# A two-layer graph attention kernel: the first x chunks cut to 2, 2, 4 and then 8 tiles, and three of them rectified at once

## The chip, the cores and the metric

One core of one Trainium2 chip. The metric is device time of the whole kernel in microseconds (us), the median of several runs. Engines are named as the profile names them: PE (TensorE), PEld (its weight loads), ACT (ScalarE), DVE (VectorE), POOL (GpSimd), SP (the queue that issues most DMAs).

## The reference

Two graph attention layers over 8192 nodes with 256 features and a dense int32 adjacency matrix of 8192 x 8192.

```
h  = relu(layernorm(x));  Wh = h @ W
e  = (Wh @ a_left)[:, None] + (Wh @ a_right)[None, :]
x1 = x + leaky_relu(softmax(where(adj, e, -inf), axis=1) @ Wh, 0.2)      # layer 0
h  = relu(layernorm(x1))
out = x1 + softmax(where(adj, leaky_relu(h@a_l + (h@a_r).T), -inf)) @ h  # layer 1
```

In layer 0 the left score falls out of the softmax, so a row of attention weights is the adjacency mask times one weight per key, exp(score of the key minus the largest score).

## The kernel before, in words

The 8192 rows of x are 64 tiles of 128. The part that the change touches is the opening of layer 0, which has four stages and ends when the largest score is known.

**Loading.** SP loads x into HV in chunks of tiles, two DMAs for each chunk (L330, every other tile each). `EDGES` holds the chunk borders: 0, 2, 8, 16, ... 64, nine chunks. Chunk c >= 4 is issued when chunk c-4 has landed. Between chunk 0 and the rest SP issues the weights W (L334), the attention row (L335) and the identity (L337), and all three count on one semaphore, `w_in`. After the chunks come six constants and one row of h. Then SP loads the adjacency matrix in quarters of a tile (L358), each when ACT has converted the quarter that was in its buffer.

**Normalising.** DVE computes `statistics(c)`: a bn_stats for each tile of the chunk (L610) and then a bn_aggr for each (L615). ACT takes the roots of the variances (`roots(c)`, L463). DVE's `scales(c)` makes 1/std (L620) and -mean/std (L623), and ACT's `relus(c)` (L477) writes relu of the normalised tile, tile by tile. ACT's order is: roots(0), relus(0), roots(1), and then for c = 2 to 8 roots(c) followed by relus(c-1), and relus(8) last. In front of relus(7) it also loads the table of Exp (L495). DVE's order is: statistics(0), scales(0), `score_columns` (L593, L595: the identity as bf16, and W times the attention row as an extra column of W), statistics(1), scales(1), statistics(2), and then statistics(c), scales(c-1) for c = 3 to 8; scales(8) stands in the loop that follows.

**Projecting.** PE runs, for t = 0 to 63, `transpose_h(t)` (L980, two transposes) and then `project(t-1)` (L989, four matmul records of 128x257, with the score as an extra column). `relus` has a copy of the transposed tile t-2 (`copy_hT`, L470) behind the relu of tile t. So ACT's order is relu t, copy t-2, relu t+1, copy t-1. DVE copies each projection out of PSUM (`take_wh(t)`, L603). Inside the statistics the copy of tile t-TAKE stands behind the bn_stats of tile t; TAKE is 24. There are three PSUM buffers for projections, so project(t) waits for take_wh(t-3). Behind the relus of tiles 28, 32, ... 56 ACT converts a quarter of adjacency (L458), eight in all. DVE folds the converted masks of two tiles into words (L642 to L656), behind take_wh(43) and take_wh(59), and PE turns them (L1001) after transpose 50 and at the end.

**Weighting.** When the last projection is copied, DVE reduces the scores, POOL finds the largest (its L424), ACT takes the exponentials (L512), and ACT and DVE make the weighted values of the 64 tiles (L519, L703). PE's first aggregation (L1016) follows this tile by tile. After that PE runs the aggregation of 64 row tiles, with conversions, folds and lists beside it. Layer 1 follows.

PE starts with two waits, on `w_in` and on `ucol_ready` (the score columns in W).

Of the kernel before, what the change touches and what calls it, by code (L numbers as in the profile page):

```python
# [35 lines left out]
def two_layer_graph_attention(nc, x, adj, w0, a0, a1, key_pos, ident, tri, caps, row_ids, self_pos, out):  # L36
# [30 lines left out]
    P = 128  # L67
    N, D = x.shape
    T = N // P
# [10 lines left out]
    Q = 4  # L80
    QC = N // Q
    QB = QC // P
    XC = 8
    EDGES = [0, 2] + list(range(XC, N // P + 1, XC))
    NCH = len(EDGES) - 1
    TAKE = 24
    XB = 4
    LAG = 5
    XL = 1
# [47 lines left out]
    with outer:  # L137
# [13 lines left out]
        with ctx:  # L151
# [99 lines left out]
            ucol_ready = sem("ucol_ready")  # L251
# [64 lines left out]
            SPARSE, DENSE = SP0, -NS  # L316

            CONVERTS = list(range(T - 2 * Q * 4 - 4, T - 4, 4))
            FOLDS = {CONVERTS[Q - 1] + 3: 0, CONVERTS[2 * Q - 1] + 3: 1}

            def offset(t):
                return SPARSE if t < NS else DENSE
# [2 lines left out]
            def _(sp):  # L325
                def load_chunk(c):
                    if c >= XB:
                        sp.wait_ge(x_in[c % XB], c // XB * 32)
                    for h in range(2):
                        sp.dma_start(H[:, EDGES[c] + h:EDGES[c + 1]:2, 0:D],  # L330
                                     x_v[:, EDGES[c] // 2:EDGES[c + 1] // 2, h, :]).then_inc(x_in[c % XB], 16)

# [117 lines left out]
            def _(act):  # L450
# [10 lines left out]
                def roots(c):  # L461
                    act.wait_ge(mv_ready, EDGES[c + 1])
                    nc.scalar.activation(std[:, EDGES[c]:EDGES[c + 1]], mv[:, EDGES[c]:EDGES[c + 1], 1],  # L463
                                         ACT.Sqrt, bias=eps[:, :]).then_inc(std_ready, 1)
# [8 lines left out]
                def relus(c):  # L473

                    act.wait_ge(nmr_ready, c + 1)
                    for t in range(EDGES[c], EDGES[c + 1]):
                        nc.scalar.activation(H[:, t, 0:D], H[:, t, 0:D], ACT.Relu,  # L477
                                             scale=rstd[:, t:t + 1],
                                             bias=nmr[:, t:t + 1]).then_inc(h_ready, 1)
                        if t >= 2:  # L480
                            copy_hT(t - 2)
                        if t in CONVERTS:
                            k = CONVERTS.index(t)
                            convert(k // Q, k // Q, [k % Q], True)

                act.wait_ge(ones_set, 1)
                nc.scalar.activation(std1[:, :], eps[:, :], ACT.Sqrt, bias=eps[:, :]).then_inc(warm, 1)
                roots(0)
                relus(0)
                roots(1)  # L490
                for c in range(2, NCH):
                    roots(c)
                    if c == NCH - 1:
                        act.wait_ge(warm, 1)
                        nc.scalar.activation(std1[:, :], eps[:, :], ACT.Exp).then_inc(warm, 1)  # L495
                    relus(c - 1)
                relus(NCH - 1)
                copy_hT(T - 2)
                copy_hT(T - 1)
# [79 lines left out]
                for j in range(NX):  # L579
                    t = last * NX + j  # L580
# [8 lines left out]
            def _(dve):  # L589
# [15 lines left out]
                def statistics(c):  # L605
                    dve.wait_ge(x_in[c % XB], 32 * (c // XB + 1))
                    if c:
                        dve.wait_ge(mv_ready, EDGES[c])
                    for t in range(EDGES[c], EDGES[c + 1]):
                        nc.vector.bn_stats(st[:, t % XC, :], H[:, t, 0:D]).then_inc(st_ready, 1)  # L610
                        if t >= TAKE:
                            take_wh(t - TAKE)
                    for t in range(EDGES[c], EDGES[c + 1]):
                        dve.wait_ge(st_ready, t + 1)
                        nc.vector.bn_aggr(mv[:, t, :], st[:, t % XC, :]).then_inc(mv_ready, 1)  # L615
# [10 lines left out]
                statistics(0)  # L626
                scales(0)
                score_columns()
                statistics(1)
                scales(1)  # L630
                dve.wait_ge(ones_set, 2)
                for c in range(2, NCH):
                    statistics(c)
                    if c > 2:
                        scales(c - 1)
                def fold(t, b, part):

# [38 lines left out]

                for t in range(T - TAKE, T - TAKE + XC - 2):
                    take_wh(t)
# [20 lines left out]
                with dve.Fori(0, T // VU) as k:  # L699
                    for j in range(VU):  # L700
                        t = k * VU + j
# [268 lines left out]
            @block.tensor  # L970
            def _(pe):
                pe.wait_ge(w_in, 16 * 3)
                pe.wait_ge(ucol_ready, 2)

                def transpose_h(t):
                    pe.wait_ge(h_ready, t + 1)
                    if t >= 2:
                        pe.wait_ge(hT_ready, t - 1)
                    for c in range(2):
                        last = nc.tensor.transpose(tps[t % 2][:, c * P:(c + 1) * P],  # L980
                                                   H[:, t, c * P:(c + 1) * P], idf[:, :])
                    last.then_inc(tr_ready, 1)

                def project(t):
                    pe.wait_ge(hT_ready, t + 1)
                    if t >= 3:
                        pe.wait_ge(wh_ready, t - 2)
                    for c in range(2):
                        last = nc.tensor.matmul(wps[t % 3][:, 0:DV], hT[:, t % 2, c, :], w_sb[:, c, :],  # L989
                                                start=(c == 0), stop=(c == 1))  # L990
                    last.then_inc(proj_ready, 1)

                def turn(t, b, reuse=True):

                    pe.wait_ge(fold_ready, t * 3 + 3)
                    if reuse:
                        pe.wait_ge(pk_ready, t - 1)
                    pe.sem_inc(masks_due, 1)
                    words = fold1[:, b, 1, :].bitcast(bf16)
                    for q in range(BQ):  # L1000
                        last = nc.tensor.transpose(turned[b].bitcast(bf16)[:, q * P:(q + 1) * P],  # L1001
                                                   words[:, q * P:(q + 1) * P], idb[:, :])
                    last.then_inc(words_ps, 1)

                def aggregate(t, b, v0_wait=False, reuse=True, turn_at=T // 16):

                    pe.wait_ge(adjT_ready, t + 1)
                    if reuse:
                        pe.wait_ge(ysb_ready, t - 1)
                    pe.sem_inc(masks_due, 1)  # L1010
                    for jb in range(T):
                        if v0_wait:
                            pe.wait_ge(v0_ready, jb + 1)
                        for s in range(2):
                            q, i, h = place(jb)
                            last = nc.tensor.matmul(acc[b][:, 0:DV], adjT_h[:, b, i, q, :, h],  # L1016
                                                    V0[:, jb, s, 0:DV], start=(jb == 0 and s == 0),
                                                    stop=(jb == T - 1 and s == 1))
                        if jb == turn_at:
                            turn(t + 1, 1 - b)  # L1020
                    last.then_inc(acc_ready, 1)

                for t in range(T):
                    transpose_h(t)
                    if t >= 1:
                        project(t - 1)
                    if t == T - 14:
                        pe.wait_ge(idb_ready, 1)
                        turn(0, 0, False)
                project(T - 1)  # L1030
                turn(1, 1, False)
                pe.wait_ge(wh_ready, T)
                pe.wait_ge(ones_set, 2)
                aggregate(0, 0, v0_wait=True, reuse=False, turn_at=None)
                aggregate(1, 1, reuse=False, turn_at=3 * T // 4)
                with pe.Fori(1, SORT // 2) as k:
                    for b in range(2):
                        aggregate(k * 2 + b, b)
                for b in range(2):
                    aggregate(SORT + b, b)  # L1040
                pe.wait_ge(const_in, 16 * 6)
                pe.wait_ge(totals_ready, 1)
                nc.tensor.matmul(kps[0][:, 0:KC], trib[:, 0:P], sums2[:, 1, :], start=True, stop=False)
                nc.tensor.matmul(kps[0][:, 0:KC], trib[:, P:2 * P], sums2[:, 0, :], start=False, stop=True)\
                    .then_inc(rank_ps, 1)
                with pe.Fori(SORT // 2 + 1, T // 2 - 1) as k:
                    for b in range(2):
                        aggregate(k * 2 + b, b)
                aggregate(T - 2, 0)
                aggregate(T - 1, 1, turn_at=None)  # L1050
                pe.wait_ge(h12_kept, 3 * T - 2)
                nc.tensor.transpose(kps[1][0:T, 0:P], h1all[:, :], idf[:, :]).then_inc(h1T_ps, 1)
# [747 lines left out]
```

## Time and profile before

| what | value |
|---|---|
| median of 3 runs | 1689.78 us (1688.65 to 1690.71) |
| the profiled execution's own time | 1692.08 us |
| its span | 1689.8 us |
| busy: PE, DVE, ACT, POOL | 1551.9, 1256.5, 989.3, 564.1 us |
| mean granted TensorE clock | 0.973 |

The span begins with the first instruction and ends with the last, and the device time of the same execution is 2.3 us longer. The opening, up to the copy of the last projection, is the first 100 us of it. Layer 0's aggregation ends near 1063 us, and layer 1 fills the rest. A timeline line gives start, duration, engine, source line, operation and count; a bracket behind it gives how long the engine sat idle before it, and what released it.

### The profile page before, as it was taken

How to read it: one execution, taken by the hardware profiler on the slowest of the kernel's cores; microseconds unless marked ns; L12 is line 12 of the kernel's file. 1: busy time of each engine (PE TensorE's matmuls, PEld its weight loads, DVE VectorE, ACT ScalarE, POOL GpSimd, SP SyncE). 2: the span in 40 equal slices, each digit the busy share in tenths (PEclk: the TensorE clock that was granted, in tenths of full speed). 3: DMA queues.
4: the chain of work that ended last, by engine and by line, in shares of the span. 5: the costliest groups of instructions: out<-in, count | busy, mean ns of one | idle time of the engine just before them, and what ended most of it. 6: DMA issues, size and time to landing. Idle time of an engine off the chain costs nothing. (4 is left out here: it accounts for less than half of the span.)

```text
span 1689.8 us, 37172 instructions
## 1 busy us (share of the span) xinstructions
PE 1551.9 (92%) x13443; PEld 1323.6 (78%) x13443; DVE 1256.5 (74%) x4759; ACT 989.3 (59%) x1514; POOL 564.1 (33%) x588
## 2 busy tenths in 40 slices
PE   6877999999999999999999999486898999989896
PEld 5645888888888888888888888374687877877685
DVE  6577998998898899887874443696866667666765
ACT  5978656665765566566666661675645445444542
POOL 0000000000000000000014453587777777777776
PEclk9998999999999999999999999798999999999998
DMA  9418989888988898898889994555444444444443
GB/s 312 170 49 331 349 303 372 320 293 317 369 312 295 332 357 307 302 373 320 341 328 380 397 363 106 176 133 156 117 133 110 133 122 131 116 138 117 125 119 106
DMA packets 141700, 406.91 MB, mean 241 GB/s; under 512 B 25857, under 2 KB 91586, under 8 KB 108834
## 3 DMA queue, kind: packets, MB, share of 16 engines
q1 hardware_dynamic: 116114, 335.11, 54.1%
q0 software_dynamic: 25488, 70.77, 14.7%
q8 instruction: 28, 0.46, 0.1%
q14 instruction: 70, 0.57, 0.1%
HBM read 365.39 MB, written 40.41 MB: 240 GB/s over the span
## 5 line engine op out<-in xcount | busy, mean ns | idle before, releaser
L1016 PE MATMUL banks<-HV,adjT 128*128 128x257 f16 x8192 | 939.6, 274 | 17.1 <-DVE adjT L673 9.4
L1016 PEld LDWEIGHTS banks<-HV,adjT 128*128 128x128 fp8e4 x8192 | 792.9, 98 | 149.0 <-DVE HV L703 23.1
L1750 PE MATMUL banks<-Vp,adjp 128*128 128x257 f16 x2304 | 450.3, 277 | 80.3 <-DVE adjp L1562 64.0
L458 ACT ACTIVATE adj_f<-adj_i 128x2048 fp8e4<-128x2048 int32 x256 | 480.1, 1898 | 5.5 <-DMA adj_i<-in_adj 5.5
L1334 POOL DMA_INDIRECT gat<-h_of_layer,rec x393 | 423.0, 1076 | 121.1 <-issue 115.6
L1750 PE MATMUL banks<-Vn,adjn 128*128 128x257 f16 x2304 | 449.7, 277 | 0.0
L1750 PEld LDWEIGHTS banks<-Vp,adjp 128*128 128x128 fp8e4 x2304 | 224.5, 98 | 124.0 <-issue 61.3
L440 POOL DMA_DIRECT2D xr<-x_after_layer x46 | 25.8, 561 | 834.1 <-DVE rank L941 772.4
L1750 PEld LDWEIGHTS banks<-Vn,adjn 128*128 128x128 fp8e4 x2304 | 227.0, 99 | 36.3
L1369 ACT ACTIVATE adjn<-h1bc,nh 128x384 fp8e5<-128x384 f32 x384 | 202.4, 603 | 0.0
L1390 ACT ACTIVATE e<-gat,hb 128x4 f32<-128x4 f32 (+3 forms) x168 | 41.2, 293 | 241.9 <-DMA gat<-h_of_layer,rec 241.9
L1623 DVE SCALAR_TENSOR_TENSOR sacc<-gat,w,sacc 128x257 f32<-128x257 f32 x347 | 157.6, 480 | 0.0
L1601 DVE TENSOR_TENSOR w<-e 128x5 f32<-128x5 f32 (+2 forms) x84 | 13.7, 163 | 166.2 <-ACT e L1390 165.9
L506 ACT ACTIVATE pk<-banks 128x512 uint16<-128x512 uint16 x64 | 37.7, 589 | 137.9 <-PE banks L1001 137.8
L670 DVE TENSOR_SCALAR adjT<-pk 128x512 uint16<-128x512 uint16 x448 | 95.1, 283 | 0.0
L710 DVE RECIPROCAL rden<-banks 128x1 f32<-128x1 f32 x64 | 10.7, 168 | 109.7 <-PE banks L1016 108.5
L989 PE MATMUL banks<-w_sb,hT 128*128 128x257 f32 x256 | 69.6, 395 | 16.0 <-ACT hT L470 15.7
L642 DVE SCALAR_TENSOR_TENSOR fold<-adj_f 128x1024 int32<-128x1024 int32 x64 | 77.2, 1207 | 7.6 <-ACT adj_f L458 7.5
L539 ACT ACTIVATE hh<-x,nmr,rstd 128x256 f32<-128x256 f32 x64 | 38.5, 601 | 61.2 <-DVE nmr L742 61.2
L533 ACT ACTIVATE std<-mv,eps 128x1 f32<-128x1 f32 x64 | 18.9, 295 | 92.7 <-DVE mv L734 92.4
L547 ACT ACTIVATE ysb<-banks,rden 128x256 f32<-128x256 f32 x64 | 29.8, 466 | 72.4 <-DVE rden L710 72.4
L989 PEld LDWEIGHTS banks<-w_sb,hT 128*128 128x128 f32 x256 | 45.2, 197 | 22.8 <-ACT hT L470 18.9
(172 smaller groups left out, 1481.9 us busy)
## 6 DMA issues: line engine op xcount, KB each, us to landing
adj_i<-in_adj SPq DMA_DIRECT2D x256, 1024.0 KB, 7.3
h_of_layer<-hh SPq DMA_DIRECT2D x64, 129.0 KB, 6.9
hs<-h_of_layer SPq DMA_DIRECT2D x64, 129.0 KB, 3.3
xt<-in_x SPq DMA_DIRECT2D x64, 128.0 KB, 7.0
packed_adj<-pk SPq DMA_DIRECT2D x64, 128.0 KB, 6.7
x_after_layer<-x SPq DMA_DIRECT2D x64, 128.0 KB, 7.1
HV<-in_x SPq DMA_DIRECT2D x14, 512.0 KB, 8.8
gat<-h_of_layer,rec POOLq DMA_INDIRECT x393
```

Source lines behind the costliest of these rows:

```text
L458: nc.scalar.activation(adj_f[:, b, q * QC:(q + 1) * QC], adj_i[:, q, :], ACT.Copy, scale=2.0, saturate=False).then_inc(conv_done, 1)
L506: nc.scalar.activation(pk[:, pb, :], turned[b].bitcast(u16), ACT.Copy).then_inc(pk_ready, 1)
L539: nc.scalar.activation(hh[:, b, 0:D], x1[:, b, :], ACT.Relu, scale=rstd1[:, bass.ds(t, 1)], bias=nmr1[:, bass.ds(t, 1)]).then_inc(hh_ready, 1)
L642: nc.vector.scalar_tensor_tensor(four, whole[:, 0:4 * GW], 1, whole[:, 4 * GW:8 * GW], ALU.logical_shift_right, ALU.bitwise_or)\
L670: last = nc.vector.tensor_scalar(adjT[:, b, i, :], pk[:, pb, :], PAIR << i, 6 - i, ALU.bitwise_and, ALU.logical_shift_left)
L989: last = nc.tensor.matmul(wps[t % 3][:, 0:DV], hT[:, t % 2, c, :], w_sb[:, c, :], start=(c == 0), stop=(c == 1))
L1016: last = nc.tensor.matmul(acc[b][:, 0:DV], adjT_h[:, b, i, q, :, h], V0[:, jb, s, 0:DV], start=(jb == 0 and s == 0), stop=(jb == T - 1 and ...
L1334: pool.indirect_dma_start(gat[:, k % NBUF, s - s0, :], None, h_d, bass.IndirectOffsetOnAxis(ap=rec[:, m, s:s + 1], axis=0))\
L1369: i = nc.scalar.activation(adjn_b[:, c % AN, jb // 2, :, jb % 2], h1bc[:, g2, :], ACT.Relu, scale=-BIG, bias=nh2[:, tiles[j]:tiles[j] + 1] ...
L1390: nc.scalar.activation(e8[:, k % 2, i, 0:s1 - s0], gat[:, k % NBUF, 0:s1 - s0, DV], ACT.Exp, scale=scale, bias=hb[:, i, m:m + 1]).then_inc ...
L1623: nc.vector.scalar_tensor_tensor(acc, x, w, acc, ALU.mult, ALU.add)\
L1750: mm = nc.tensor.matmul(bank[2 * i + part][:, 0:DV], m[:, i * P:(i + 1) * P], V[:, j, s, 0:DV], start=(j == 0 and s == 0), stop=(j == T - ...
```

## The change

The chunk borders become 0, 2, 4, 8, 16, ... 64, ten chunks. `DIRECT` is 3: chunks 0, 1 and 2 (tiles 0 to 7) go through statistics, roots, scales and relus before the next chunk is looked at, on ACT and on DVE. From chunk 3 on ACT runs roots(c) ahead of relus(c-1), and DVE statistics(c) ahead of scales(c-1). `TAKE` becomes 18, so that the copy of projection t-18 stands behind the bn_stats of tile t, and the first fold stands behind take_wh(46). PE no longer waits for the score columns before the first transpose, but before the first projection.

```diff
-    EDGES = [0, 2] + list(range(XC, N // P + 1, XC))
+    EDGES = [0, 2, XC // 2] + list(range(XC, N // P + 1, XC))
     NCH = len(EDGES) - 1
-    TAKE = 24
+    DIRECT = 3
+    TAKE = 18
...
-            FOLDS = {CONVERTS[Q - 1] + 3: 0, CONVERTS[2 * Q - 1] + 3: 1}
+            FOLDS = {T - TAKE: 0, CONVERTS[2 * Q - 1] + 3: 1}
...
-                roots(0)
-                relus(0)
-                roots(1)
-                for c in range(2, NCH):
+                for c in range(DIRECT):
+                    roots(c)
+                    relus(c)
+                for c in range(DIRECT, NCH):
                     roots(c)
                     if c == NCH - 1:
                         act.wait_ge(warm, 1)
                         nc.scalar.activation(std1[:, :], eps[:, :], ACT.Exp).then_inc(warm, 1)
-                    relus(c - 1)
+                    if c > DIRECT:
+                        relus(c - 1)
                 relus(NCH - 1)
...
                 score_columns()
-                statistics(1)
-                scales(1)
+                for c in range(1, DIRECT):
+                    statistics(c)
+                    scales(c)
                 dve.wait_ge(ones_set, 2)
-                for c in range(2, NCH):
+                for c in range(DIRECT, NCH):
                     statistics(c)
-                    if c > 2:
+                    if c > DIRECT:
                         scales(c - 1)
...
                 pe.wait_ge(w_in, 16 * 3)
-                pe.wait_ge(ucol_ready, 2)
...
                         pe.wait_ge(wh_ready, t - 2)
+                    if t == 0:
+                        pe.wait_ge(ucol_ready, 2)
```

## Rows read from the trace of the kernel before

**Rows 1.** windows: stretch, length, busy us of PE, PEld, DVE, ACT, POOL (records), PE clock, DMA share, GB/s

```profile
70.00:80.00 10.00, 7.19 (x38) 5.52 (x37) 5.04 (x13) 9.77 (x18) 0.00 (x0) 1.00 0.40 129
...
100.00:110.00 10.00, 3.98 (x21) 2.21 (x19) 8.55 (x33) 6.22 (x16) 0.37 (x1) 0.71 0.00 0
```

**Rows 2.** timeline, PE, start of layer 0: start, duration, operation, [idle before it <- releaser]

```profile
16.85 2.08 PE L989 MATMUL banks<-w_sb,hT 128*128 128x257 f32 x4 [8.01 <-ACT hT L470]
...
22.88 1.03 PE L989 MATMUL banks<-w_sb,hT 128*128 128x257 f32 x4
...
27.24 1.03 PE L989 MATMUL banks<-w_sb,hT 128*128 128x257 f32 x4
```

**Rows 3.** timeline, ACT, same stretch

```profile
5.27 1.09 ACT L477 ACTIVATE HV<-HV,nmr,rstd 128x256 f32<-128x256 f32 x2 [0.51 <-DVE nmr L623]
...
15.74 0.30 ACT L463 ACTIVATE std<-mv,eps 128x8 f32<-128x8 f32 x1 [3.75 <-DVE mv L615]
15.94 0.59 ACT L477 ACTIVATE HV<-HV,nmr,rstd 128x256 f32<-128x256 f32 x1
16.43 0.36 ACT L470 ACTIVATE hT<-banks 128x256 f32<-128x256 f32 x1
...
33.35 0.59 ACT L477 ACTIVATE HV<-HV,nmr,rstd 128x256 f32<-128x256 f32 x1
```

**Rows 4.** timeline, DVE, same stretch

```profile
3.45 0.75 DVE L610 BATCH_NORM_STATS2 st<-HV 128x6 f32<-128x256 f32 x2 [3.45 <-DMA HV<-in_x]
...
5.07 0.16 DVE L623 SCALAR_TENSOR_TENSOR nmr<-mv,rstd 128x2 f32<-128x2 f32 x1
...
7.57 0.08 DVE L595 DVE_READ_ACCUMULATOR2_ANT w_sb<- 128x1 f32 x1
9.19 2.06 DVE L610 BATCH_NORM_STATS2 st<-HV 128x6 f32<-128x256 f32 x6 [1.54 <-issue]
...
15.08 0.62 DVE L615 BATCH_NORM_AGGREGATE mv<-st 128x2 f32<-128x6 f32 x8
...
28.31 0.43 DVE L603 COPY HV<-banks 128x257 f32<-128x257 f32 x1 [0.33 <-PE banks L989]
28.65 0.63 DVE L615 BATCH_NORM_AGGREGATE mv<-st 128x2 f32<-128x6 f32 x8
...
29.48 0.17 DVE L623 SCALAR_TENSOR_TENSOR nmr<-mv,rstd 128x8 f32<-128x8 f32 x1
```

**Rows 5.** timeline, PE, later part of the projections

```profile
53.41 1.03 PE L989 MATMUL banks<-w_sb,hT 128*128 128x257 f32 x4
...
55.52 1.14 PE L989 MATMUL banks<-w_sb,hT 128*128 128x257 f32 x4 [0.85 <-ACT hT L470]
...
74.22 1.03 PE L989 MATMUL banks<-w_sb,hT 128*128 128x257 f32 x4
...
76.23 1.14 PE L989 MATMUL banks<-w_sb,hT 128*128 128x257 f32 x4 [0.75 <-ACT hT L470]
...
78.79 1.14 PE L989 MATMUL banks<-w_sb,hT 128*128 128x257 f32 x4 [1.21 <-ACT hT L470]
```

**Rows 6.** timeline, ACT, before and after the table load in front of tile 48

```profile
73.61 0.29 ACT L463 ACTIVATE std<-mv,eps 128x8 f32<-128x8 f32 x1
...
75.33 0.58 ACT L477 ACTIVATE HV<-HV,nmr,rstd 128x256 f32<-128x256 f32 x1
```

**Rows 7.** timeline, DVE: a fold, and the last copy of a projection

```profile
73.46 1.21 DVE L642 SCALAR_TENSOR_TENSOR fold<-adj_f 128x1024 int32<-128x1024 int32 x1
...
76.10 0.75 DVE L603 COPY HV<-banks 128x257 f32<-128x257 f32 x2
...
99.97 0.43 DVE L603 COPY HV<-banks 128x257 f32<-128x257 f32 x1 [0.63 <-PE banks L989]
```

**Rows 8.** timeline, SP, issues of x chunks and of adjacency quarters

```profile
3.11 19.94 SPq L330 DMA_DIRECT2D HV<-in_x  x16
...
83.48 50.67 SPq L358 DMA_DIRECT2D adj_i<-in_adj  x3
```

## The prediction

> **What bounds the kernel now.** I read the windows of the opening first, for where PE is idle: it is short of work at the start, in the conversions (7.19 us busy of the ten from 70 us) and in the step to the weighted values (3.98 of the ten from 100 us) [rows 1]. The timelines say what PE waits for. Its first projection starts at 16.85, after 8.01 us of idleness that ended with ACT's copy of transposed tile 0 [rows 2]. That copy, at 16.43 [rows 3], stands behind the relu of tile 2, and that relu behind roots(2), which needs the statistics of tiles 8 to 15: their bn_aggr runs from 15.08 for 0.62 us [rows 4]. So the start is set by order on ACT and DVE, not by loading: tiles 0 and 1 were rectified from 5.27 on [rows 3].
>
> From the fourth projection (22.88) PE is the bound: four tiles from 22.88 to 27.24, 1.09 us each. The first three took 6.03 us (16.85 to 22.88) where 3.27 would do, and a projection's matmuls ran 2.08 us against 1.03: twice the time, so I read 1.2 GHz there and 2.4 GHz behind it [rows 2]. In the conversions PE waits for ACT, 0.85 us in front of 55.52 [rows 5]. DVE waits for PE at a take (0.33 us in front of 28.31), and this is slack today: take 7, the last in statistics(4), starts at 28.31 and the scales that follow are made at 29.48, while ACT reaches tile 16, which needs them, at 33.35 [rows 3, 4]. The slack is 33.35 - 29.48 - 0.20 = 3.7 us, 0.20 being the step from 5.07 to 5.27.
>
> Everything after the opening hangs on its end, the last take at 99.97 [rows 7]: largest score, weights, the values tile by tile, and with them the next loads. SP stands in an adjacency issue from 83.48 for 50.67 us, three issues in all [rows 8], because its buffer is free only when ACT converts again after the values. So I carry a shift of the end through one for one.
>
> **The change, part by part.**
>
> *Chunks 1 and 2 direct.* After the change DVE goes from the score columns (last record 7.57 + 0.08 = 7.65) to the statistics of tiles 2 and 3. From bn_stats to relu, chunk 0 took 3.45 to 5.27 = 1.82 us for two tiles [rows 3, 4]. So relu 2 starts at 7.7 + 1.8 = 9.5. The copy of tile 0 follows 0.49 later and the projection 0.42 after that (15.94 to 16.43 to 16.85): 10.4, against 16.85. **Gain 6.4 us.** This needs chunk 1 in by 7.65. No row shows a 256 KB chunk there. Bounds: all 768 KB of the old chunk were in by 9.19 [rows 4], which would cost 1.5 us; for the other end, earlier landing gains nothing, as DVE is busy until 7.65. I take 7.65, as a third of those bytes comes first. Two more issues on SP stand among sixteen that take 19.94 us, 1.25 each at most, [rows 8] with other chunks in flight; the adjacency quarters behind them are needed only by ACT's first conversion, behind the relu of tile 28. Cost 0.
>
> The Trainium skill, page "DMA: Bandwidth & Descriptors", Rules for kernel authors, advises to coalesce transfers, since each has a fixed part of about 2.0 us (its Anatomy section). Were that paid in series by both new chunks, the gain would be an estimated 2.4 us. No row shows it paid by a chunk with others in flight. The first chunk's data were in use at 3.45 [rows 4], which leaves room for such a part once.
>
> Later steps of the start keep pace: two tiles took 1.62 us from bn_stats to scales, and two more add a third of 2.06 and a quarter of 0.62 [rows 4], so four take 2.5; relu 4 is at about 12.2, statistics(3) ends near 15.3, and the first take, three bn_stats later at 16.3, is just in time for projection 3 at 10.4 + 6.0 = 16.4.
>
> *PE's wait for the score columns moved.* PE's first transposes start about 1.1 us earlier, but project(0) waits for the copy near 10.0 anyway. Worth 0; the copy is the cover.
>
> *TAKE 24 to 18.* This closes a loop. Statistics(c) for tiles 8k to 8k+7 now ends with take(8k-11). On ACT roots(c), which needs its bn_aggr, and on DVE scales(c-1), stand behind it, and relu(8k-8) behind both; copy 8k-10 is behind that relu, and project(8k-10) behind the copy. So the projection of tile 8k-10 waits for the copy-out of the one just before it, through four engine hops, where TAKE 24 left six tiles of slack. Six tiles are 6.5 us, and the slack is 3.7. The trip from the start of project(8k-11) to that of the next:
>
> - project to take: 27.24 to 28.31, 1.07
> - take to scales: 28.31 to 29.48, 1.17
> - scales to relu: 0.20; relu to copy: 0.49; copy to project: 0.42
>
> Together 3.35 us instead of 1.09 [rows 2 to 4]: **2.26 us lost** each time. It happens ahead of tiles 8, 16, 24, 32 and 40: 5 x 2.26 = 11.3. Between two gaps PE does seven more projections at its own pace, so it catches up nothing. Relu 8 starts 2.44 after project(5), at 18.6 + 1.07 + 1.17 + 0.20 = 21.0.
>
> *Ahead of tile 48* the Exp table lies in the loop: project to take 1.07, take to bn_aggr 0.34, bn_aggr to root 0.66 (15.08 to 15.74), root to relu 1.72 (73.61 to 75.33, with the table between), then 0.49 and 0.42: 4.70, where 74.22 to 76.23 = 2.01 stands now [rows 3 to 6]. **Lost 2.7 us.**
>
> *Conversions behind tiles 32 and 40* now follow directly on a copy that PE waited for. Where that is so today, behind tile 48, PE's step is 76.23 to 78.79 = 2.56 us; elsewhere PE lags a little and the step is 53.41 to 55.52 = 2.11 [rows 5]. **Lost 2 x 0.45 = 0.9.** After an idle stretch PE's matmuls take 1.14 us in place of 1.03: five new ones, **0.5**.
>
> *The last chunk.* scales(9) is behind take 51, and tile 56 needs it. Its scales come 1.07 + 0.34 + 0.28 + 0.20 = 1.9 us after the start of project(51), and in that time PE has one or two tiles of 1.09 in hand, since ACT runs two tiles ahead of it: 0. If the cover is gone, 0.8 (1.9 less 1.09). The moved fold takes 2.64 us (73.46 to 76.10) [rows 7] behind take 46; PE's turn comes three projections later, 2.56 + 2 x 1.09 = 4.7 us. 0; without that cover 2.6.
>
> Sum: -6.4 + 11.3 + 2.7 + 0.9 + 0.5 = **+9.0 us**. Against the profiled execution (1692.08, span 1689.8) that is 1701.1; its own time lies 2.3 above the median, and from the median of 1689.78 I say 1698.8.
>
> **Rivals.**
>
> *Faster: the loop doesn't bind.* If the takes in the statistics were in before ACT needs scales(c-1), only the start would change: 1689.8 - 6.4 = 1683.4. It sits in DVE's queue at take(8k-11) and decides by whether the slack there (3.7 us today) stays above zero. For it: DVE's waits cost nothing today. Against: six tiles at 1.09 exceed 3.7. The slack would have to be 2.8 us more than I read. 0.08.
>
> *Slower still: PE's clock falls in the new gaps.* Idle stretches of 0.75 and 1.21 us left the full clock (1.00 in the window from 70 us); in the window from 100 us, PE idle for 6.0 of ten, it was 0.71, so partly 1.2 GHz [rows 1, 5]. The new gaps are about 2.3 us, and 3.5 ahead of tile 48. A start at 1.2 GHz costs 6.03 - 3.27 = 2.8 us. Once, at tile 48: 1701.6. All six times: 1698.8 + 16.6 = 1715.4. All six 0.06; the single one is in the main case's range. The Trainium skill, page "TensorE: Matmul & The Clock Gate", Why this matters for your kernels, says that idle gaps between bursts return the engine to its half rate. By that rule the longest gap is the one at risk.
>
> *No change: absorbed.* If adjacency loads or layer 1 set the time whatever the opening does, 1689.8. Against: the loads are themselves released by ACT. 0.04.
>
> *The chunk doesn't land early.* With the start only 4.9 us sooner, 1700.3, inside the main case.
>
> **How the numbers follow.** The loop case has 0.82. Its own range: chunk 1 late +1.5; half-rate stretch a tile or two longer or shorter at the start, 1.1 each; clock lost once +2.8; run to run about 1. That gives 1695 to 1702.5. I widen it a little: 1694.5 to 1703 leaves out the other three cases, 0.18. A measurement of this kernel tells 0.2% (3.4 us) from no change. Slower by more: 0.82 + 0.06 = 0.88; within 0.2%: the 0.04 of absorption and 0.01 of the first rival's 0.08; faster: its other 0.07.
>
> **What would show it.** First projection near 10.4; PE idle about 2.3 us before the projections of tiles 6, 14, 22, 30, 38 and 3.5 before 46, released by ACT's copy; ACT waiting for DVE in front of tiles 8, 16, ...; last take near 109 instead of 99.97. If PE runs through at 1.09 from tile 3 on, the loop argument is wrong; if PE shows 2.1 us a tile after a gap, the clock rival is right; if the take is late but the end isn't, absorption.

## The result

The changed kernel takes 1708.59 us (median of 4 runs, 1707.31 to 1710.56) against 1689.39 for the kernel before: ratio 1.0111, interval 1.0096 to 1.0126, so 19.2 us slower. The forecast was slower by 9.0, 1698.8, with a range up to 1703.0. The ratio is that of the record, which is not simply the quotient of the two medians. The sign and the loop hold, the size doesn't: the time lies outside the range.

The profiled execution took 1707.51 us, its span 1705.6. First its timeline of PE, in the same columns as [rows 2] and [rows 5]. PE's projections are numbered from 0, the one at 9.87; only those in question are shown.

```profile
9.87 2.08 PE L993 MATMUL banks<-w_sb,hT 128*128 128x257 f32 x4 [2.36 <-ACT hT L471]
...
18.07 2.05 PE L993 MATMUL banks<-w_sb,hT 128*128 128x257 f32 x4 [2.58 <-DVE HV L605]
...
20.34 1.34 PE L993 MATMUL banks<-w_sb,hT 128*128 128x257 f32 x4
...
21.74 1.03 PE L993 MATMUL banks<-w_sb,hT 128*128 128x257 f32 x4
...
25.10 1.14 PE L993 MATMUL banks<-w_sb,hT 128*128 128x257 f32 x4 [2.11 <-ACT hT L471]
...
36.18 1.14 PE L993 MATMUL banks<-w_sb,hT 128*128 128x257 f32 x4 [2.11 <-ACT hT L471]
...
47.27 1.15 PE L993 MATMUL banks<-w_sb,hT 128*128 128x257 f32 x4 [2.11 <-ACT hT L471]
...
48.64 1.92 PE L993 MATMUL banks<-w_sb,hT 128*128 128x257 f32 x4
...
61.16 1.37 PE L993 MATMUL banks<-w_sb,hT 128*128 128x257 f32 x4 [2.11 <-ACT hT L471]
...
63.71 2.08 PE L993 MATMUL banks<-w_sb,hT 128*128 128x257 f32 x4 [0.76 <-ACT hT L471]
...
77.03 1.14 PE L993 MATMUL banks<-w_sb,hT 128*128 128x257 f32 x4 [2.10 <-ACT hT L471]
...
79.59 2.08 PE L993 MATMUL banks<-w_sb,hT 128*128 128x257 f32 x4 [1.20 <-ACT hT L471]
...
94.25 1.14 PE L993 MATMUL banks<-w_sb,hT 128*128 128x257 f32 x4 [3.46 <-ACT hT L471]
...
96.81 2.08 PE L993 MATMUL banks<-w_sb,hT 128*128 128x257 f32 x4 [1.20 <-ACT hT L471]
...
119.07 1.11 PE L993 MATMUL banks<-w_sb,hT 128*128 128x257 f32 x4 [0.32 <-DVE HV L605]
```

The first line answers to 16.85 of [rows 2]: the start is 6.98 us earlier. The lines with 2.10 or 2.11 us idle are projections 6, 14, 22, 30 and 38, the one with 3.46 is projection 46. All six were forecast, at their places and with that releaser. Two things had no term in the forecast's sum. Projection 3 (18.07) waits 2.58 us for a copy of DVE. And projection 3 itself, and one to three projections behind each of 47.27, 61.16, 77.03 and 94.25, take 1.9 to 2.1 us instead of 1.03, that is, PE is at 1.2 GHz; this was only a rival.

DVE around the first two of these waits, as in [rows 4]:

```profile
7.15 0.75 DVE L612 BATCH_NORM_STATS2 st<-HV 128x6 f32<-128x256 f32 x2
...
9.81 1.41 DVE L612 BATCH_NORM_STATS2 st<-HV 128x6 f32<-128x256 f32 x4 [0.90 <-DMA HV<-in_x]
...
13.16 2.71 DVE L612 BATCH_NORM_STATS2 st<-HV 128x6 f32<-128x256 f32 x8 [0.86 <-DMA HV<-in_x]
...
16.51 1.08 DVE L612 BATCH_NORM_STATS2 st<-HV 128x6 f32<-128x256 f32 x3
17.51 0.41 DVE L605 COPY HV<-banks 128x257 f32<-128x257 f32 x1
...
22.81 0.43 DVE L605 COPY HV<-banks 128x257 f32<-128x257 f32 x1 [0.33 <-PE banks L993]
23.15 0.63 DVE L617 BATCH_NORM_AGGREGATE mv<-st 128x2 f32<-128x6 f32 x8
...
23.97 0.17 DVE L625 SCALAR_TENSOR_TENSOR nmr<-mv,rstd 128x8 f32<-128x8 f32 x1
...
120.21 0.42 DVE L605 COPY HV<-banks 128x257 f32<-128x257 f32 x1 [0.62 <-PE banks L993]
```

Chunk 1 was there when DVE asked for it (7.15). Chunks 2 and 3 were not: DVE sat idle 0.90 and 0.86 us for x. The first copy (17.51) stands behind three bn_stats of chunk 4 (16.51) and is what projection 3 waited for. The copy at 22.81 is number 5, and bn_aggr, 1/std and -mean/std follow it. Then ACT:

```profile
23.82 0.30 ACT L464 ACTIVATE std<-mv,eps 128x8 f32<-128x8 f32 x1 [2.66 <-DVE mv L617]
24.18 0.60 ACT L478 ACTIVATE HV<-HV,nmr,rstd 128x256 f32<-128x256 f32 x1
24.68 0.36 ACT L471 ACTIVATE hT<-banks 128x256 f32<-128x256 f32 x1
```

The root waited 2.66 us for DVE's bn_aggr, relu 8 follows, the copy of transposed tile 6 at 24.68, and projection 6 at 25.10. From projection 5 (21.74) to 6 are 3.36 us; the forecast added up 3.35.

The windows of the opening, columns as in [rows 1]:

```profile
20.00:30.00 10.00, 7.89 (x42) 6.58 (x41) 5.85 (x24) 5.85 (x15) 0.00 (x0) 0.95 1.09 352
30.00:40.00 10.00, 7.89 (x44) 6.54 (x43) 6.15 (x25) 6.29 (x16) 0.11 (x1) 1.00 0.84 315
...
60.00:70.00 10.00, 8.08 (x27) 6.18 (x28) 3.29 (x10) 7.33 (x13) 0.00 (x0) 0.66 0.33 120
...
80.00:90.00 10.00, 9.99 (x39) 7.80 (x39) 4.27 (x12) 6.23 (x13) 0.00 (x0) 0.71 0.49 184
```

PE's clock is 1.00 from 30 us on for ten us, with an idle stretch of 2.11 us in them, and down to 0.66 and 0.71 later. PE looks fully busy from 80 us (9.99 of ten) because much of its work there runs at half rate. At the start of the program I go by durations alone: in the kernel before, the window from 10 to 20 us shows a granted clock of 1.00, and the projection at 16.85 in it took 2.08 us all the same.

**Where the 20 us of the opening are.** The last copy starts at 120.21 instead of 99.97: +20.2. In steps of PE's timelines of the two kernels:

| stretch | before, us | after, us | difference | forecast |
|---|---|---|---|---|
| start of projection 0 | 16.85 | 9.87 | -7.0 | -6.4 |
| projection 0 to 3 | 6.03 | 8.20 | +2.2 | 0 |
| 3 to 5 | 2.18 | 3.67 | +1.5 | 0 |
| 5 to 6, and the same ahead of tiles 16, 24, 32, 40 | 5 x 1.09 | 5 x 3.36 | +11.3 | +11.3 |
| 45 to 46 | 2.01 | 4.70 | +2.7 | +2.7 |
| between those, from 6 to 45, and 46 to the end | | | +9.5 | +1.4 |
| sum | | | +20.2 | +9.0 |

The last difference is +20.24 less the rows above it. Of its 9.5 us, 1.8 lie between projections 22 and 29, 2.7 between 30 and 37, 2.7 between 38 and 45 and 2.2 between 46 and 54.

**Behind the opening.** POOL's first reduction of layer 1 marks where layer 0 ends. Before and after:

```profile
1070.91 0.38 POOL L1321 PARTITION_ALL_REDUCE red<-red_in  x1 [37.83 <-DVE red_in L1472]
```

```profile
1091.43 0.38 POOL L1325 PARTITION_ALL_REDUCE red<-red_in  x1 [37.79 <-DVE red_in L1476]
```

That is +20.5 for +20.2 at the last copy, so nothing was absorbed in layer 0. In the kernels below this mark moved by the shift of the last copy to within 0.9 us, except in the one with filled waits (12.9 for 10.6). From there to the end of the span the profiled execution of before took 618.9 us and this one 614.2. The same code took 611.4 in another run of the kernel before with one constant changed, so single times scatter by several us in layer 1, and below I read the opening from the trace (start of the last copy) beside each time.

### The profile page after: what moved, and what is told of

It is laid out like the page before. It is cut to its first block and busy times, and to the rows that moved or that the text cites. A ratio compares the mean times of both kernels' runs of the same rounds, so it can differ in the third digit from the quotient of the medians.

```text
span 1705.6 us, 37180 instructions
## 1 busy us (share of the span) xinstructions
PE 1563.4 (92%) x13443; PEld 1330.4 (78%) x13443; DVE 1257.8 (74%) x4761; ACT 989.9 (58%) x1515; POOL 560.9 (33%) x588
## 5 line engine op out<-in xcount | busy, mean ns | idle before, releaser
L1338 POOL DMA_INDIRECT gat<-h_of_layer,rec x393 | 417.4, 1062 | 121.6 <-issue 115.3
L993 PE MATMUL banks<-w_sb,hT 128*128 128x257 f32 x256 | 80.0, 441 | 24.8 <-ACT hT L471 21.9
L993 PEld LDWEIGHTS banks<-w_sb,hT 128*128 128x128 f32 x256 | 51.0, 222 | 34.4 <-ACT hT L471 26.2
```

What stands on the lines that cost most here:

```text
L1338: pool.indirect_dma_start(gat[:, k % NBUF, s - s0, :], None, h_d, bass.IndirectOffsetOnAxis(ap=rec[:, m, s:s + 1], axis=0))\
```

## The experiments

Each kernel is told by its difference from the kernel before or from the changed one. "Last copy" is 99.97 us before and 120.21 after the change. They ran in three groups, each on another chip with the kernel before beside it: TAKE 18 alone, TAKE 21, the filled waits and the score columns (kernel before 1689.84 us), TAKE 19 and 20, DIRECT 4 and the chunks of before (1689.57), and the two others (1688.29). So kernels of different groups are compared by their ratios and their traces rather than by their times.

### The loop alone

```diff
-    TAKE = 24
+    TAKE = 18
-            FOLDS = {CONVERTS[Q - 1] + 3: 0, CONVERTS[2 * Q - 1] + 3: 1}
+            FOLDS = {T - TAKE: 0, CONVERTS[2 * Q - 1] + 3: 1}
```

in the kernel before.

> The kernel before with TAKE 18 and the fold behind take 46, nothing else of the change. Theory (loop of copy-out, statistics, scales, relu, copy, project, and PE's clock falling in the gaps): the start stays at 16.85, six gaps of about 2.1 to 3.5 us appear ahead of the projections of tiles 6, 14, 22, 30, 38, 46; +14 us from the gaps and +1 from the conversions, and up to 10 more from the clock: 1705 to 1715. Rival (the small chunks and their late landing cost the time): no change, 1689.5 within 1.5.

1708.02 us, ratio 1.0110 (1.0087 to 1.0133). PE's timeline:

```profile
17.25 2.08 PE L989 MATMUL banks<-w_sb,hT 128*128 128x257 f32 x4 [7.71 <-ACT hT L470]
...
27.53 1.14 PE L989 MATMUL banks<-w_sb,hT 128*128 128x257 f32 x4 [2.10 <-ACT hT L470]
...
66.14 2.08 PE L989 MATMUL banks<-w_sb,hT 128*128 128x257 f32 x4 [0.87 <-ACT hT L470]
...
95.91 2.08 PE L989 MATMUL banks<-w_sb,hT 128*128 128x257 f32 x4 [3.45 <-ACT hT L470]
```

The start is at 17.25, projection 6 waits 2.10 us, projection 46 waits 3.45, and PE runs at half rate there (95.91) and at 66.14. The last copy is at 121.4. So TAKE 18 by itself costs what the whole change costs. The small chunks are not the cause. They don't help much either: with them the start is 7.4 us earlier and the last copy only 1.2 (121.39 and 120.21), where the forecast let the whole gain at the start through.

### The loop opened, tile by tile

```diff
-    TAKE = 18
+    TAKE = 19      (a_take19), 20 (a_take20), 21 (a_take21)
```

in the changed kernel.

> The changed kernel with TAKE 19. Loop theory: each tile of slack is worth 1.09 us, so the idle stretches ahead of projections 6, 14, 22, 30, 38 shrink from 2.11 to 1.02, and the one ahead of 46 from 3.46 to 2.4. If PE's clock falls only behind the longer stretches, the opening is then 6 x 1.09 = 6.5 us shorter and a good part of the 10 us of half rate goes too: 1695 to 1701. Rival (the gaps are not set by the copy-out): gaps stay 2.1, 1708.

> The changed kernel with TAKE 20. Loop theory: two tiles are 2.18 us of slack against a trip that is 2.26 too long: idle stretches of about 0.1 us or none, no fall of the clock after tile 8, within 2 us of the kernel with TAKE 21: 1687 to 1690. Rival (the two need not be in step): anything near 1695.

> The changed kernel with TAKE 21 instead of 18. Theory: three tiles of slack (3.3 us) close the 2.26 us gaps, so all six go, and with them the drops of the clock; the first take comes three bn_stats later than with 18, so PE waits in front of projection 3 a little longer, and the start is only some 3 to 4 us earlier than in the kernel before: 1685 to 1688. Rival (small chunks, or the direct order, cost the time): 1700 or more.

| TAKE | idle ahead of 14, 22 | ahead of 46 | last copy | time, us | ratio (interval) |
|---|---|---|---|---|---|
| 18 | 2.11 | 3.46 | 120.2 | 1708.59 | 1.0111 (1.0096 to 1.0126) |
| 19 | 1.01 | 2.36 | 109.2 | 1700.02 | 1.0051 (1.0032 to 1.0070) |
| 20 | none | 1.28 | 103.1 | 1691.17 | 1.0008 (0.9995 to 1.0022) |
| 21 | none | 0.76 | 99.2 | 1687.46 | 0.9979 (0.9968 to 0.9990) |

A tile of distance takes 1.10 us out of each wait, as expected, until it is gone; with 21 the 0.76 ahead of 46 is that of the kernel before [rows 5]. TAKE 20 came out 1 us slower than its range, and its trace has a fall of the clock that I had ruled out: behind idle stretches of 1.28 and 1.21 us projection 47 takes 2.08 us (80.38), and 46 to 54 is 1.5 us longer than with TAKE 21. From 18 to 19 the opening gains 11.0 us where six waits of 1.1 make 6.6. The rest is clock: the stretches 22 to 29, 30 to 37 and 38 to 45, behind the waits, are 4.5 us shorter. And with TAKE 21 projection 3 still waits:

```profile
10.06 2.08 PE L993 MATMUL banks<-w_sb,hT 128*128 128x257 f32 x4 [2.66 <-ACT hT L471]
...
19.00 2.05 PE L993 MATMUL banks<-w_sb,hT 128*128 128x257 f32 x4 [3.04 <-DVE HV L605]
...
98.05 1.11 PE L993 MATMUL banks<-w_sb,hT 128*128 128x257 f32 x4 [0.32 <-DVE HV L605]
```

The start is 6.8 us earlier than before, the end 0.8. The wait of 3.04 us ahead of projection 3 and the half rate around it (2.05, and 1.92 and 1.90 behind it) have eaten the rest: from projection 0 to 6 are 15.3 us here and 9.3 in the kernel before.

> The kernel before with TAKE 21, nothing else. The slack of 3.7 us read in front of tile 16 less three tiles of 1.09 leaves 0.4: no new idle stretch on PE, last copy within 0.5 us of 99.97, time unchanged within 1.5 us. Rival (slack smaller in front of a later tile, as in front of 48 where the table is loaded): an idle stretch over 1.3 us in front of projection 46 and 1 to 3 us slower.

The kernel before with `TAKE = 21`: 1689.69 us, ratio 1.0012 (1.0000 to 1.0023), last copy at 99.93 (before 99.97), waits as in the kernel before, and 0.76 ahead of 46. The slack of 3.7 us holds three tiles and not six, as forecast. It was read a little short: TAKE 20 leaves no wait ahead of 14 and 22 either, and with TAKE 18 alone six tiles cost 2.27 us, so up to PE the slack is 6 x 1.09 - 2.27 = 4.3 us.

### The clock

PE is given transposes in its waits whose results nobody reads.

```diff
+                FILL = {3: 18, 6: 16, 14: 16, 22: 16, 30: 16, 31: 8, 38: 16, 39: 8, 46: 28, 47: 8}
+
+                def fill(n):
+                    for i in range(n):
+                        nc.tensor.transpose(bank[2][:, 0:P], idf[:, :], idf[:, :])
+
                 def project(t):
+                    fill(FILL.get(t, 0))
                     pe.wait_ge(hT_ready, t + 1)
```

> The changed kernel with transposes that nobody reads put on PE where it waits: 18 ahead of projection 3, 16 ahead of projections 6, 14, 22, 30, 38, 28 ahead of 46, and 8 ahead of 31, 39, 47, at 0.11 us each at full clock, so that they end inside the waits. Theory (PE's clock falls because of the waits, about 10 us of the 19): the waits of the others stay, projections run 1.03 us again instead of 2.08, and the whole takes 1698 to 1701. Rival (the slow projections have another cause, or the loop alone is the cost and I miscounted it): 1708 or more.

1699.82 us, ratio 1.0047 (1.0029 to 1.0064), as the theory had it. PE around projection 6, then windows as for the changed kernel:

```profile
20.37 1.03 PE L1000 MATMUL banks<-w_sb,hT 128*128 128x257 f32 x4
...
21.46 1.91 PE L990 MATMUL banks<-idf 128*128 128x128 f32 x16
23.73 1.14 PE L1000 MATMUL banks<-w_sb,hT 128*128 128x257 f32 x4 [0.37 <-ACT hT L471]
```

```profile
20.00:30.00 10.00, 9.63 (x60) 8.28 (x59) 6.41 (x25) 6.48 (x17) 0.00 (x0) 1.00 1.09 353
30.00:40.00 10.00, 9.64 (x60) 8.30 (x59) 6.16 (x25) 6.29 (x16) 0.11 (x1) 1.00 0.82 301
...
60.00:70.00 10.00, 8.81 (x51) 7.23 (x49) 5.10 (x16) 7.32 (x15) 0.00 (x0) 1.00 0.61 223
...
80.00:90.00 10.00, 9.27 (x63) 8.11 (x64) 4.72 (x18) 7.19 (x15) 0.00 (x0) 1.00 0.36 116
```

From projection 5 (20.37) to 6 (23.73) are 3.36 us as without the filling: the loop is untouched. The clock is 1.00 in every window of ten us up to the last projection, no projection behind the first two is slow, and the last copy starts at 110.58 instead of 120.21, 9.6 us earlier. The table above leaves 1.5 us for 3 to 5 and 9.5 - 1.4 = 8.1 for the others: 9.6. Compared directly, the filled kernel is 1.4 us shorter from 3 to 5, 1.7 from 22 to 29 and 2.2 in each of 30 to 37, 38 to 45 and 46 to 54. This is the price of the clock, and it is about half of what the change costs. With the clock up, the stretches of the table's last row but one differ from the kernel before by 1.3 us where 1.4 was forecast.

### The wait for the score columns

```diff
                 pe.wait_ge(w_in, 16 * 3)
+                pe.wait_ge(ucol_ready, 2)
...
-                    if t == 0:
-                        pe.wait_ge(ucol_ready, 2)
```

> The changed kernel with PE's wait for the score columns back in front of the first transpose. Both theories: first transposes 0.6 us later (7.1 instead of 6.4), first projection still behind ACT's copy at 9.5; no change, 1708.6 within 1.5. If the moved wait mattered it would be 1 us or more slower.

Inconclusive in time: 1705.29 us, but its four runs lie between 1697.86 and 1713.27 (ratio 1.0086, 1.0052 to 1.0121). The trace of one execution says more: first projection at 9.50 behind ACT's copy (9.87 with the wait moved), so the moved wait gained nothing at the start. The last copy starts 0.5 us earlier than in the changed kernel.

### The late first copy

```diff
+    EARLY = {12: 0, 14: 1, 16: 2}
...
-                        if t >= TAKE:
+                        if t in EARLY:
+                            take_wh(EARLY[t])
+                        elif t - TAKE > max(EARLY.values()):
                             take_wh(t - TAKE)
```

in the changed kernel, TAKE 18 kept.

> The changed kernel, TAKE 18 kept, with copies 0, 1, 2 behind bn_stats 12, 14, 16. Theory (projection 3 waited for copy 0, which stood behind bn_stats 18): the 2.6 us in front of projection 3 go and it starts near 15.3, but tile 8 is still held by DVE until about 22, so PE's stretch moves to the front of projection 6 and is some 4 us there; the loop stays as it is for the other tiles. Only 1 to 2 us of the opening come back: 1706 to 1709. Rival (the late first copy costs its 2.6 us and the half rate behind it outright): 1703 to 1705.

1704.38 us, ratio 1.0109 (1.0080 to 1.0138) to a kernel before that ran 1688.29 beside it. By this ratio it can't be told from the changed kernel (1.0111).

```profile
17.84 1.11 PE L996 MATMUL banks<-w_sb,hT 128*128 128x257 f32 x4 [0.30 <-DVE HV L606]
...
22.84 1.56 PE L996 MATMUL banks<-w_sb,hT 128*128 128x257 f32 x4 [3.67 <-ACT hT L472]
...
92.42 2.08 PE L996 MATMUL banks<-w_sb,hT 128*128 128x257 f32 x4 [1.20 <-ACT hT L472]
```

Projection 3 starts at 15.12 with no wait, and 3.67 us of idleness stand ahead of projection 6, as I expected. That one is 2.3 us earlier than in the changed kernel (22.84 against 25.10). But the last copy is 4.4 us earlier (115.82), and the time is below my range and inside the rival's, though the ratio doesn't bear out so large a gain. The other 2.1 us in the opening lie behind projection 6, where the same waits cost less by the clock: 6 to 13 is 1.7 us longer than in the changed kernel, 30 to 37 is 1.6 shorter and 38 to 45 2.2 (1.14 at 77.40, where the changed kernel has 2.08 at 79.59). Why they did is open.

### The early start with nothing in its way

The changed kernel with DIRECT 4, DVE's wait for `ones_set` one loop earlier, and:

```diff
-    DIRECT = 3
-    TAKE = 18
+    DIRECT = 4
+    TAKE = 21
+    EARLY = {10: 0, 12: 1, 15: 2, 16: 3, 17: 4, 18: 5, 20: 6, 22: 7, 24: 8, 26: 9, 28: 10}
```

with the same lines in `statistics` as above.

> The changed kernel with DIRECT 4 (tiles 8 to 15 rectified directly too), the first eleven copies placed by hand behind bn_stats 10, 12, 15, 16, 17, 18, 20, 22, 24, 26, 28, and TAKE 21 from copy 11 on. Theory: the wait ahead of projection 3 (2.6 to 3.0 us, for the copy of projection 0) goes, and with it the half rate of projections 3 to 5; projection 3 starts near 15.5 and 6 near 19; last copy 5 to 7 us earlier than in the kernel before: 1683 to 1685, the fastest. Rival (the early start is taken back by the later loads or by DVE, whatever the copies do): 1687 or more.

1685.94 us (12 runs), ratio 0.9976 (0.9963 to 0.9989): the lowest median here, faster than both kernels, though only 3.6 us below the kernel before, and by its interval not to be told from TAKE 21 above (0.9979).

```profile
10.44 2.08 PE L996 MATMUL banks<-w_sb,hT 128*128 128x257 f32 x4 [3.12 <-ACT hT L472]
...
92.23 1.11 PE L996 MATMUL banks<-w_sb,hT 128*128 128x257 f32 x4 [0.32 <-DVE HV L606]
```

Projection 3 starts at 15.21, the last projection at 92.23 instead of 98.83: the whole early start, 6.4 us, is kept, in the opening. The last copy is 6.6 us earlier than in the kernel before (93.38 against 99.97). In the profiled execution this reaches the end: layer 1 begins 6.9 us earlier, and the span is 1681.8 against 1689.8. The median time, 1685.94, is just above what I expected and below the rival's. The medians show only 3.6 us; with single times from 1678.83 to 1688.57 I can't say where the other 3 us are.

> The chunks of before (0, 2, 8, ...) with the direct order for two chunks and TAKE 21, so that tiles 2 to 7 are one chunk. First projection near 13 instead of 10, but what follows waits for DVE's statistics and the first copies, so the last copy comes at the same time as with the small chunks and TAKE 21: within 1 us of that kernel. Rival (the early first projection is worth what it shows): 3 us slower than that kernel.

The chunks of before (`EDGES = [0, 2]` and on), `DIRECT = 2`, `TAKE = 21`: 1687.18 us, ratio 0.9984 (0.9974 to 0.9994).

```profile
13.49 2.08 PE L993 MATMUL banks<-w_sb,hT 128*128 128x257 f32 x4 [5.91 <-ACT hT L471]
...
95.66 1.11 PE L993 MATMUL banks<-w_sb,hT 128*128 128x257 f32 x4 [0.32 <-DVE HV L605]
```

It starts 3.4 us later than with the small chunks and TAKE 21 and ends 2.4 us earlier (95.66 against 98.05), which neither theory expected; the times are within 1 us of each other, as I had put it, but for another reason. PE has no wait between its first projection and the conversions here, while the earlier start there ran into the wait ahead of projection 3 and back to half rate. So with TAKE 21 the split of chunk 1 is worth less than nothing in the opening. With the first copies placed early and DIRECT 4 the last projection starts 3.4 us ahead of this one (92.23 against 95.66); what the early copies would give with the chunks of before was not run, so how much of the 3.4 us is the split's isn't shown.

## Why the prediction was wrong in size

**Right.** *The gain at the start*: 6.4 forecast, 7.0 measured. Chunk 1 was in by 7.15, so no fixed part of a transfer was paid in series ahead of it. Had it been, as I worked out beside the advice of the Trainium skill to coalesce ("DMA: Bandwidth & Descriptors", Rules for kernel authors), an estimated 2.4 us would have been left. The page measured its 2.0 us on DMAs issued by GpSimd, and these are issued by SP. *The loop*: 3.35 us a trip forecast, 3.36 measured, five times, and 4.70 forecast and measured the sixth time, with the table in it. TAKE 18 alone reproduces the loss, and each tile of TAKE takes 1.1 us out of each wait. *The score columns*: nothing, by the trace. *The shift goes through layer 0 one for one*: +20.5 for +20.2. *The small terms*, 0.9 behind the conversions and 0.5 behind idle stretches: 1.3 together, in the kernel with filled waits.

**Wrong, first: the clock.** The sum of +9.0 us had no term for PE's clock; it stood only among the rivals ("PE's clock falls in the new gaps"). That is the step that failed. I gave six falls at 2.8 us each a chance of 0.06, and let a single fall of 2.8 us widen the range, because idle stretches up to 1.21 us had left the clock up and the shortest that I knew to go with a clock below 1.00 was of 6 us, ahead of the first aggregation of the kernel before:

```profile
106.17 6.71 PE L1016 MATMUL banks<-HV,adjT 128*128 128x257 f16 x32 [6.02 <-DVE HV L703]
```

Between those rows there was nothing, and I put 2.3 us with the lower one. The measured price is 9.6 us, in five falls (at projection 3 and behind 22, 30, 38 and 46) at 1.4 to 2.2 each, where I had priced one at 2.8. So a fall was priced too high, and the count of none or one was far too low. The case should have carried much more chance, with counts from one to six. The rule of the Trainium skill that I set beside it ("TensorE: Matmul & The Clock Gate", Why this matters for your kernels) pointed the right way; I read from it that only the longest stretch was at risk, and the runs show that shorter ones were too.

**Wrong, second: projection 3.** That the first take comes just in time for projection 3 was the other step: forecast 16.3 and 16.4, measured 17.51 and 18.07. PE started 0.5 us earlier than forecast and projection 2 ran at full rate already (1.03 us, where the one in the kernel before took 1.53), so PE asked at 15.5; and chunks 2 and 3 landed when DVE was already idle, 0.90 and 0.86 us, where I had let DVE run from one to the next. Why they came that late was not tried. Two steps on the edge, each with a zero. That is 2.2 us, and the first fall of the clock went with its wait of 2.58 us: with that wait filled to 0.45 us projection 3 took 1.11 us.

The opening was 11.2 us longer than forecast: 8.1 and 1.5 of clock and 2.2 ahead of projection 3, less 0.6 at the start. So the gain of 6.4 us at the start and the costs of TAKE 18 don't simply add, as the sum had them: with TAKE 21 the start at 10.06 met a wait of 3.04 us at projection 3, and the start at 13.49 met none.

The other rivals fell: nothing was absorbed, the loop binds, and chunk 1 landed early.

## What to carry to other kernels

When a copy-out stands in an in-order queue ahead of something that its own producer waits for, count the distance in tiles against the slack in the trace, and count PE's idle stretches too: each may cost once as a wait and once more at half rate behind it. An earlier start is worth only what the next in-order wait lets through; here, with TAKE 21, 7 us at the first projection were 0.8 at the last until the copies were moved with it. Where rows bracket a stretch (1.2 us left the clock up, a clock below 1.00 went with 6), a new value between them belongs on both sides of the forecast, and the runs here show that even the lower bound isn't safe.

## What the runs showed that I had not expected

Idle stretches of the same length, 2.11 us, left PE's clock up twice (25.10, 36.18) and not the third time (47.27) in one execution. In the kernel with TAKE 19 two stretches of 1.02 and 1.20 us, one projection apart, were followed by a projection of 2.08 us (57.76), and two others of the same lengths (69.32, 71.88) were not:

```profile
55.20 1.14 PE L993 MATMUL banks<-w_sb,hT 128*128 128x257 f32 x4 [1.02 <-ACT hT L471]
...
57.76 2.08 PE L993 MATMUL banks<-w_sb,hT 128*128 128x257 f32 x4 [1.20 <-ACT hT L471]
...
69.32 1.14 PE L993 MATMUL banks<-w_sb,hT 128*128 128x257 f32 x4 [1.02 <-ACT hT L471]
...
71.88 1.14 PE L993 MATMUL banks<-w_sb,hT 128*128 128x257 f32 x4 [1.20 <-ACT hT L471]
```

So the length of one stretch doesn't decide it here, and which falls come differs from kernel to kernel with the same waits: behind the 2.1 us ahead of projection 38 the changed kernel has a fall and the one with three early copies has none. Filling the longer waits to 0.3 to 0.5 us, with those of 0.6 to 0.9 us left as they were, kept the clock up throughout. What exactly decides was not tried.
